# Scratch quarters laid out in 2 KB chunks, and two output stores and the wide adapter rows issued after a load has landed

## The reference

```
x = x + ffn0(cond0(x))     # cond0: x @ w_eff.T, w_eff a quantized weight plus a low-rank term
x = x + ffn1(cond1(x))     # ffn: x @ W.T plus a top-2-of-8 mixture of rank-16 adapters
# cond1: base = x @ W1.T + bias; low = x @ A[id].T; base + scale[id] * (low @ B[id].T)
#        one adapter id for each sequence of 64 tokens
```

## Time and profile before

| | |
|---|---|
| median of 3 runs | 913.54 us (912.75 to 913.76) |
| the profiled execution | 914.59 us, its span 912.8 us |
| granted PE clock over the span | 0.997 |
| PE busy | 904.0 us, 99% |
| DVE, ACT, POOL busy | 616.2, 312.7, 145.3 us |
| DMA | 191.51 MB, mean 210 GB/s; 265 GB/s from 437 us on |

### The profile page before, as it was taken

The page is one execution under the profiler, slowest core; times in us unless marked ns, Lnnn a source line. Parts: engine busy times, 40 slices in busy tenths (PEclk is TensorE's granted clock), DMA queues, the critical chain, the costliest instruction groups (busy, mean ns, idle before and its releaser), DMA issues.

```text
span 912.8 us, 13364 instructions
## 1 busy us (share of the span) xinstructions
PE 904.0 (99%) x4672; PEld 789.1 (86%) x4672; DVE 616.2 (68%) x1311; ACT 312.7 (34%) x502; POOL 145.3 (16%) x298
## 2 busy tenths in 40 slices
PE   8999999999999999999999999999999999999998
PEld 8999998888998878888888888888888788888886
DVE  6789899776587959976465566566566566566563
ACT  6579788411224424232322222222222222212220
POOL 0100010111001001414213113113113113113110
PEclk9999999999999999999999999999999999999999
DMA  8523330665612032556887887887887887887875
GB/s 338 189 95 122 119 124 24 234 210 190 141 50 93 4 135 90 212 217 226 277 277 253 285 272 259 286 270 260 286 269 261 285 267 260 290 266 263 286 226 182
DMA packets 63090, 191.51 MB, mean 210 GB/s; under 512 B 10664, under 2 KB 13100, under 8 KB 61104
## 3 DMA queue, kind: packets, MB, share of 16 engines
q1 hardware_dynamic: 52448, 159.19, 50.8%
q0 software_dynamic: 10432, 31.35, 11.4%
q10 hardware_dynamic: 144, 0.13, 0.1%
HBM read 158.93 MB, written 32.23 MB: 209 GB/s over the span
## 4 chain that ended last, share of the span: by engine, by line
PE 88%; DMA 7%; DVE 3%; ACT 1%; issue 0%; SPq 0%; DVEq 0%; ACTq 0%
PE bank L852 26%; PE bank L518 13%; PE bank L519 13%; PE bank L520 13%; DMA t_lo<-t_scratch 5%; PE bank L826 5%; PE bank L835 5%; PE bank L663 2%; PE bank L909 2%; PE bank L923 2%; PE bank L922 2%; PE bank L924 2%; PE bank L580 1%; DMA x_raw<-xq 1%; DMA m_raw<-m1t 1%; DMA w<-e_scratch 1%
## 5 line engine op out<-in xcount | busy, mean ns | idle before, releaser
L852 PE MATMUL bank<-g_hi,xs 128*128 128x512 f32 x448 | 145.2, 395 | 0.0
L852 PE MATMUL bank<-t_hi,xs 128*128 128x512 f32 x336 | 113.4, 396 | 1.6 <-DMA t_lo<-t_scratch 1.4
L489 POOL DMA_DIRECT2D p1sel<-p_scratch x128 | 65.3, 510 | 280.2 <-issue 280.2
L852 PEld LDWEIGHTS bank<-g_hi,xs 128*128 128x128 f32 x448 | 83.2, 188 | 16.5
L954 ACT ACTIVATE xs<-x_raw 128x1024 fp32r<-128x1024 f32 x60 | 62.0, 1056 | 81.3 <-PE bank L852 55.7
L852 PE MATMUL bank<-g_lo,xs 128*128 128x512 f32 x224 | 88.3, 394 | 0.0
L1277 DVE TENSOR_TENSOR xs<-x_raw,xs 128x1024 fp32r<-128x1024 f32 x60 | 75.2, 1274 | 17.2 <-ACT xs L954 16.7
L518 PE MATMUL bank<-gx,xs 128*128 128x304 f32 x256 | 77.4, 302 | 0.0
L520 PE MATMUL bank<-gx,xs 128*128 128x304 f32 x256 | 77.4, 302 | 0.0
L519 PE MATMUL bank<-gx,xs 128*128 128x304 f32 x256 | 77.3, 302 | 0.0
L852 PEld LDWEIGHTS bank<-t_hi,xs 128*128 128x128 f32 x336 | 62.0, 188 | 16.6 <-DMA t_lo<-t_scratch 4.4
(11 more groups left out here) (321 smaller groups left out, 2064.2 us busy)
## 6 DMA issues: line engine op xcount, KB each, us to landing
t_hi<-t_scratch SPq DMA_DIRECT2D x82, 512.0 KB, 4.5
t_lo<-t_scratch SPq DMA_DIRECT2D x82, 512.0 KB, 5.9
x_raw<-xq SPq DMA_DIRECT2D x16, 1024.0 KB, 6.9
out<-ost SPq DMA_DIRECT2D x64, 256.0 KB, 4.7
p1sel<-p_scratch POOLq DMA_DIRECT2D x64, 192.0 KB, 4.7
w_raw<-wall SPq DMA_DIRECT2D x16, 512.0 KB, 4.3
w<-e_scratch SPq DMA_DIRECT2D x6, 1024.0 KB, 5.1
ea<-e_scratch POOLq DMA_DIRECT2D x8, 644.0 KB, 4.2
```

The source lines that it names most:

```text
L489: pool.dma_start(f(p1sel[b][STK * s:STK * s + STK, cs]), p1_dram[bass.ds(i * STK, STK), cs]).then_inc(sems[b], 16)
L852: mm = nc.tensor.matmul(bk[j][:], l[:, c, :], m[:, c, :], start=first and c + k == 0, stop=c + k == KH + 1, skip_group_check=True)
```

## The change

There are three edits. First, `t_scratch` gets the shape (4, 2, 2, 2, P, 512): the two chunks of a half lie one behind the other, each as 128 rows of 2,048 bytes without a gap. Stores and loads of the quarters go by 2,048 contiguous bytes in DRAM instead of 4,096. Second, SP waits, behind the issue of load t4, until both halves of t4 have landed, before it issues the two output stores for banks 2 and 1. Third, POOL waits for the same landing before it issues the wide adapter rows of the tile.

```
 def store_t(k, n): ...
-    sp.dma_start(t_dram[k - 1, h, 0, :, 0:D].rearrange("p (c n) -> p c n", n=512),
+    sp.dma_start(t_dram[k - 1, h, 0].rearrange("c p n -> p c n"),
                  f(t_hi[:, 2 * h:2 * h + 2, :])).then_inc(st_t[h], 16)
 def load_t(k, used): ...
     sp.dma_start(f(t_hi[:, 2 * h:2 * h + 2, :]),
-                 t_dram[k - 1, h, 0, :, 0:D].rearrange("p (c n) -> p c n", n=512)).then_inc(ld_t[h], 16)
+                 t_dram[k - 1, h, 0].rearrange("c p n -> p c n")).then_inc(ld_t[h], 16)
...
             for tau in range(REG, NT2):
                 n = tau - REG
                 load_t(4, 6 * n + 1)
+                for h in range(2):
+                    sp.wait_ge(ld_t[h], 32 * (3 * n + 1))
                 store_out(tau - 1, (2, 1))
                 load_t(3, 6 * n + 3)
...
                 if tau:
                     pool.wait_ge(low_mm, tau)
+                if tau >= REG:
+                    for h in range(2):
+                        pool.wait_ge(ld_t[h], 32 * (3 * (tau - REG) + 1))
                 load_p1(tau, ld_p1w, slice(0, D))
...
-    args.append(nc.dram_tensor("t_scratch", (4, 2, 2, P, NM1), F32, kind="Internal").ap())
+    args.append(nc.dram_tensor("t_scratch", (4, 2, 2, 2, P, 512), F32, kind="Internal").ap())
```

More of the change, by code:

```diff
@@ L401, in store_t @@
                     sp.wait_ge(t_lo_s, 2 * n + h + 1)
-                    sp.dma_start(t_dram[k - 1, h, 0, :, 0:D].rearrange("p (c n) -> p c n", n=512),
+                    sp.dma_start(t_dram[k - 1, h, 0].rearrange("c p n -> p c n"),
                                  f(t_hi[:, 2 * h:2 * h + 2, :])).then_inc(st_t[h], 16)
-                    sp.dma_start(t_dram[k - 1, h, 1, :, 0:D].rearrange("p (c n) -> p c n", n=512),
+                    sp.dma_start(t_dram[k - 1, h, 1].rearrange("c p n -> p c n"),
                                  f(t_lo[:, 2 * h:2 * h + 2, :])).then_inc(st_t[h], 16)
@@ L410, in load_t @@
                     sp.dma_start(f(t_hi[:, 2 * h:2 * h + 2, :]),
-                                 t_dram[k - 1, h, 0, :, 0:D].rearrange("p (c n) -> p c n", n=512)).then_inc(ld_t[h], 16)
+                                 t_dram[k - 1, h, 0].rearrange("c p n -> p c n")).then_inc(ld_t[h], 16)
                     sp.dma_start(f(t_lo[:, 2 * h:2 * h + 2, :]),
-                                 t_dram[k - 1, h, 1, :, 0:D].rearrange("p (c n) -> p c n", n=512)).then_inc(ld_t[h], 16)
+                                 t_dram[k - 1, h, 1].rearrange("c p n -> p c n")).then_inc(ld_t[h], 16)
             def store_out(tau, banks):
@@ L433, in _ @@
                     sp.dma_start(f(g[:, 2 * h:2 * h + 2, 512:D]),
-                                 t_dram[1, h, hl, :, 0:D].rearrange("p (c n) -> p c n", n=512)).then_inc(ld_t2, 16)
+                                 t_dram[1, h, hl].rearrange("c p n -> p c n")).then_inc(ld_t2, 16)
             load_x(3)
```

## The result

The changed kernel takes **1000.31 us** (median of 4 runs, 993.04 to 1006.54) against 913.65 us for the kernel before, measured beside it. The ratio is 1.0958, with a 95% interval of 1.0923 to 1.0992. The direction was forecast, the size was not: 20.5 us were expected, some 87 came. The four runs differ with their granted clock, 0.979 in the fastest and 0.959 in the slowest, and it is the slowest that was profiled.

A forecast was written before the change was run, and what follows sets the result against it. PE bounds the kernel; t3 has 7.0 us to land. 6.5 + 2.2 + 0.3 - 0.3 = 8.7 us, so 1.7 us wait in 14 tiles, 23.8, less 3.3 at t4: +20.5 us, 934 us; range 911 to 949.

The forecast's parts named there:

- t3 has room enough: Rival: t3 lands within 7.0 us of its issue, so the kernel wins the 3.3 us, 910.2 us; chance 0.20.
- the two cancel: Rival: t3's wait of 0.1 to 0.35 us a tile offsets the 3.3 us won, 912 to 915 us; chance 0.08.
- PE waited nowhere at `low_terms`: Rival: wide rows land too late for `low_terms`, costing 1.1 us a tile if t3 is in time, 926 us; chance 0.07.
- Rows of 2,048 bytes: Rival: rows without a gap are read a tenth slower, quarters take 0.6 us more, 952 us; chance 0.07.
- The wide rows: Term: 0.79 million bytes moved beside load t3 make its last transfer 2.2 us later; ends 0.7 and 3.4.
- The stores: Term: two output stores ahead of load t3 in SP's queue push t3 by 0.3 us; ends 0 and 1.2.
- The chunks: Term: loading quarters by 2,048 instead of 4,096 bytes shortens a load by 0.3 us; ends 0 and -0.6.
- The gain at t4: Term: without stores behind it t4 lands in time in nearly all tiles, saving 3.3 us in all.
- the wait at step 72: Sign: a wait on `t_lo<-t_scratch` at step 72 in all fourteen tiles, together above 15 us.
- t1's landing falls from 8.2: Sign: t1's last transfer lands in less than 8.2 us, towards 6.5, since the wide rows have left it.
- tiles are 35 to 36.5 us long: Sign: each tile's length in the changed profile, where one without a wait took 34.00 us before.
- the wait on t4 is gone: Sign: PE no longer waits for t4 at chunk 2, step 36.

The follow-up runs named there:

- e1: Kernel before with only the scratch layout changed to 2,048-byte rows, both new waits left out: 915.18 us against 912.0.
- e3: Kernel before with only the wait on POOL, ahead of the wide adapter rows: 975.02 us against 912.0.
- e7: Kernel before, with the wide rows issued by SP behind t4's landing, ahead of load t3 in the same queue: 938.98 us against 912.66.
- e9: Kernel before, with the wide rows issued by ACT on its own hardware queue behind t4's landing: 973.95 us against 912.27.
- e2: Kernel before with only the wait on SP, ahead of the two output stores: 915.05 us against 912.0.
- e4: Kernel before with both waits, the scratch kept in 4,096-byte rows: 994.13 us against 912.0.
- e8: Kernel before with the two output stores moved behind the landing of t3: 912.99 us against 912.66.
- e5: Changed kernel with 18 needless products on PE between chunk 1 and chunk 2 of t3: 989.44 us against 912.66 for the kernel before.
- e6: Kernel before with the wait on POOL, loading only half the columns of the wide rows from tile 3 on: 931.76 us against 912.66.
- e12: Changed kernel with 9 needless products on PE between chunk 1 and chunk 2 of t3: 982.44 us against 912.27 for the kernel before.

## Why the prediction was wrong in size

**What bounds the kernel: right.** t3 with 7.0 us and a need of 6.5 was the point that decided, and the wait moved there. The four rivals to the forecast that were named do not hold. "t3 has room enough" and "the two cancel" fall with the ratio. PE waited nowhere at `low_terms`. Rows of 2,048 bytes were read about as well as the others (e1).

**The sum failed in three of its terms and lacked a fourth.**

*The wide rows, "at 358 GB/s, 2.2 us", measured 4.0 (e3).* This is the step that failed first. The bytes were divided by the rate of t3, and the wide rows do not move at that rate: alone in SP's queue they moved at 203 to 256 GB/s (e7), 3.4 us for all. The kernel before had shown it. From 568.2 to 570 the wide rows are nearly alone in the DMA engines, on POOL's queue:

```profile
q0 software_dynamic: 95, 0.30, 68.6%
```

0.30 million bytes in 1.8 us at a share of 0.686 is some 240 GB/s at full share, an estimate, and 3.2 us for all the rows; the sum would have given +34.5 us and 948. t1's landing beside the wide rows pointed the same way: twice its 1.7 us gives 3.4, which I kept as an end and did not take. The Trainium skill, page DMA: Bandwidth & Descriptors, section on queues, rings and completion order, has the engines go round over the queues that have work. That says who gets the share, and the runs agree that t3 pays: 4.0 us, whether the second queue is POOL's (e3) or ACT's (e9).

*The stores, "I take 0.3", measured 0.55 alone (e2),* inside the bounds, and 1.3 beside the rows (e3 to e4), at their upper end. *The chunks, "-0.3", measured -0.25 at t3 and +0.3 at t4 (e1):* as a whole a loss of 0.4%; beside rows and stores t3 lands 0.5 us sooner with them (11.8 to 11.3). The rate over four chosen microseconds of the t2 load did not carry over. The Trainium skill, page DMA: Bandwidth & Descriptors, section on why small descriptors are slow, gave by the prediction's estimate a load 0.1 us longer; that has the sign of the loss in e1.

*The gain at t4, "-3.3 us", was about nothing.* e2 and e8 moved t4's landing by 0.35 us only, where it would have needed a full one, and the waits on `t_lo` in e8 fell by 0.8 us in all. I had read the difference between 7.75 for t4 and 6.5 for t3 as the work of the stores. Most of it is not. In the changed kernel t4 is still waited for, 5.0 us in six tiles.

*The range was narrower than the terms.* The ends of the terms give t3's landing as 6.5 + 0.7 + 0 - 0.6 = 6.6 to 6.5 + 3.4 + 1.2 - 0 = 11.1 us, so waits of 0 to 4.1 us a tile. The prediction took 0.5 and 3 as its ends and gave no reason. Its own upper end is 14 x 4.1 - 3.3 = +54, 968 us.

With what the runs measured, t3 lands after 6.5 + 4.0 + 1.3 - 0.5 = 11.3 us. It alone accounts for 11.3 - 7.0 = 4.3 us of waiting in each of fourteen tiles, 60 us, against 55.1 that PE stands still longer and 1.7 x 14 = 23.8 forecast. The form of the sum was right and its term mis-sized. It had no term for t3's first half, for which PE waits 5.5 of those 55.1 us.

*The clock was not in the sum at all:* it is about 32 of the 36.9 us that PE is busy longer (e5). The forecast took a wait to cost its own length. In the tiles of the kernel before PE stood still for 0.7 us at most at a time, and its granted clock stayed at 1.00 in all of them. In the changed kernel it stood still for 2.4 to 4.0 us ahead of chunk 2 of t3 (PEld's waits, which begin sooner, are up to 4.4), and in all fourteen tiles the clock went to 0.50, for 3 to 7 us. In between it is no plain matter of length: in e7, with waits of 0.7 to 1.9 us, the clock fell in one tile of fourteen, and in e3, with 1.5 to 4.1, in nine, behind one of 2.2 us but not behind one of 3.2. e5 shows the link by filling the wait. The Trainium skill, page TensorE: Matmul & The Clock Gate, section on HAM oscillation, tells of such a kernel, in which each wait for a transfer throws the engine back to its lower clock. The trace agrees, and the forecast should have carried it as the price of a longer wait: it makes the loss steep once the wait is long, and is why even 968 us would have been too low.

**The signs that were named:** the wait at step 72 is in the tiles and far above 15 us, right; t3 takes 8 us or more, right; t1's landing falls from 8.2, right and further than forecast, to 4.7; the stores are issued just ahead of load t3, right; "tiles are 35 to 36.5 us long", wrong, 40.8 in the mean; "the wait on t4 is gone", wrong, 5.0 us of it stand there, and t4's landing stays at 7.6, above the 7.5 that was named as the sign that the stores had not made it late.

## What to carry to other kernels

Before a transfer is moved out of the way of one late load, list for each load how long it takes and how long it has; the next in the row may have less to spare than the one to be helped. Price a transfer that is moved in front of another at the rate that transfers of its own kind show in the trace while the engines are busy with them, not at the rate of the one that it delays: 230 GB/s against 358 here. Add up the ends of the terms, and let the range reach them or say why it does not. And where a wait on the matrix engine may grow to several microseconds, add to it the products behind it at half the clock: here 36.9 / 14 = 2.6 us a tile for 55.1 / 14 = 3.9 us more of standing still.

## What the runs showed of the hardware

The wide rows, which are four transfers into 48 partitions with 4,096 bytes in each, moved at 203 to 256 GB/s with one queue at work, and the quarters, into 128 partitions with the same 4,096 bytes in each, at 370 to 412 GB/s right behind them in the same queue (e7). Beside each other on two queues the two together moved at 281 (POOL's, e3) and 254 (ACT's, e9). With half the bytes in each row the window read 337 (e6). The share was 1.00 at 229 GB/s and 1.02 at 406, so a full share does not tell how much is being moved. What makes the rows slow, the 48 partitions or something else about them, was not tried.

Nine needless products, 2.1 us of work, in a wait of four microseconds brought the mean clock from 0.959 to 0.993 and the kernel from 1000 to 982 us (e12).
